# A graph kernel's count matrix: one table word per cell, and source one-hots made two units ahead

## The reference

```python
edge_index = jnp.stack([src, dst])
edge_index_t = jnp.stack([src, dst], axis=1)
x = _layernorm(x + _L0_gnn_ref(x, L0_gnn_W, L0_gnn_b, src, dst), axis=-1)
x = _layernorm(x + _L1_gnn_ref(x, edge_attr_128, edge_index_t, ...), axis=-1)
x = _layernorm(x + _L2_gnn_ref(x, edge_index, ...), axis=-1)
x = _layernorm(x + _L3_gnn_ref(x, src, dst, ...), axis=-1)
```

## Time and profile before

| | us |
|---|---|
| median of 3 runs | 8967.54 |
| lowest and highest run | 8958.18 to 8971.82 |
| profiled execution, whole time | 8958.67 |
| profiled execution, span of the core | 8956.9 |
| stage b, from its first VectorE operation to the end of loop two | 1383 to 3050 |
| loop one (32 turns) | 1450 to 2602 |
| loop two (16 lines) | 2602 to 3050 |

### The profile page before, as it was taken

How to read it: one execution, slowest core, us unless ns; L and a number is a source line. 1 busy time by engine, 2 the same in 40 slices (tenths; PEclk the granted TensorE clock), 3 DMA queues, 4 the chain that set the end, 5 groups by cost and what they waited for, 6 DMA issues and landing times. The chain is left out here.

```text
span 8956.9 us, 148669 instructions
## 1 busy us (share of the span) xinstructions
PE 6419.9 (72%) x40358; PEld 4410.9 (49%) x40359; DVE 4659.5 (52%) x13045; ACT 1832.2 (20%) x2602; POOL 3401.7 (38%) x3460
## 2 busy tenths in 40 slices
PE   0366503666666589999967777767777599968999
PEld 0255402444443245555546666656666355534555
DVE  6877745666766522222257777777777501022111
ACT  1222102333344310100013333223333100000000
POOL 0777776666663000000046666466666100000000
PEclk6688857888888799999989999889999799979999
DMA  0122202222223156777732222122222266635666
GB/s 16 46 70 72 62 1 61 89 85 85 92 92 79 50 166 175 185 177 187 191 74 50 50 50 51 43 53 50 50 51 50 74 188 190 191 101 164 192 190 182
DMA packets 871577, 901.11 MB, mean 101 GB/s; under 512 B 421539, under 2 KB 820226, under 8 KB 864867
## 3 DMA queue, kind: packets, MB, share of 16 engines
q1 hardware_dynamic: 753541, 637.16, 25.8%
q0 software_dynamic: 109664, 179.92, 8.9%
q10 hardware_dynamic: 8064, 80.29, 2.3%
HBM read 722.84 MB, written 93.87 MB: 91 GB/s over the span
## 5 line engine op out<-in xcount | busy, mean ns | idle before, releaser
L1919 POOL DMA_INDIRECT d_row_ring<-table_att,src_at x1664 | 1581.3, 950 | 819.3 <-issue 490.0
L2428 PE MATMUL psum<-e_a_ring,e_parts 128*128 128x448 bf16 x8232 | 1578.0, 353 | 82.9 <-DVE e_parts L2510 75.7
L2428 PEld LDWEIGHTS psum<-e_a_ring,e_parts 128*128 128x128 bf16 x8232 | 806.4, 98 | 823.9 <-issue 87.5
L775 POOL DMA_INDIRECT b_row_ring<-edge_attr,b_entry x896 | 894.9, 999 | 603.4 <-SPq L752 363.3
L794 PE MATMUL psum<-b_hot 128*128 x2920 | 672.7, 373 | 593.6 <-DVE b_hot L976 519.1
L353 POOL DMA_INDIRECT listed<-a_record,a_slot_no x832 | 866.0, 1041 | 314.6 <-issue 272.0
L1327 PE MATMUL psum<-c_a_ring,c_parts 128*128 128x448 bf16 x4116 | 811.6, 356 | 43.1 <-DMA c_a_ring<-adjacency 38.5
L1944 PE MATMUL psum<-edges_out,edges_in 128*128 128x120 f32 x4896 | 713.2, 307 | 179.9 <-ACT edges_in L2010 160.4
L1944 PEld LDWEIGHTS psum<-edges_out,edges_in 128*128 128x128 f32 x4896 | 661.0, 217 | 225.5 <-DVE edges_out L2103 203.9
L794 PEld LDWEIGHTS psum<-b_hot 128*128 x2920 | 293.8, 101 | 947.4 <-issue 826.7
L1960 PE MATMUL psum<-edges_out,edges_in 128*128 128x132 f32 x4896 | 651.2, 288 | 113.7 <-DVE edges_out L2157 113.7
(11 more groups left out here) (426 smaller groups left out, 7686.4 us busy)
## 6 DMA issues: line engine op xcount, KB each, us to landing
e_a_ring<-adjacency SPq DMA_DIRECT2D x1372, 224.0 KB, 2.8
c_a_ring<-adjacency SPq DMA_DIRECT2D x686, 224.0 KB, 2.9
adjacency<-b_line ACTq DMA_DIRECT2D x49, 1568.0 KB
a_cum<-edge_attr SPq DMA_DIRECT2D x103, 512.0 KB
d_row_ring<-table_att,src_at POOLq DMA_INDIRECT x1664
b_row_ring<-edge_attr,b_entry POOLq DMA_INDIRECT x896
listed<-a_record,a_slot_no POOLq DMA_INDIRECT x832
e_a_left<-adjacency_left SPq DMA_DIRECT2D x28, 224.0 KB, 3.2
```

The lines of the kernel that those rows point to most:

```text
L775: pool.indirect_dma_start(out=row_ring[:, u % 4, g, 0:D], out_offset=None, in_=a["edge_attr_128"], in_offset=bass.IndirectOffsetOnAxis(ap= ...
L1919: pool.indirect_dma_start(out=row_ring[:, u % 4, g, :], out_offset=None, in_=table_att[layer], in_offset=bass.IndirectOffsetOnAxis(ap=src_ ...
L2428: mm = nc.tensor.matmul(psum[:, 2 * (turn % 2) + v, 0:WIN], parts[:, piece, s, :], a_ring[:, s % SEVEN, v * WIN:(v + 1) * WIN], start=(s = ...
```

## The change

VectorE's share of stage b is rewritten in four points; TensorE, ScalarE, GpSimd and SyncE keep their instructions.

1. Two operations on one partition put the running count, shifted left by 19 bits, and the code of row 0 together into row 1 of `cell_row`. `spans_of` reads row 1 and takes column, number and count from one word; `befores` is no longer read by VectorE.
2. The source one-hots are made two pairs ahead: both pairs of `is_src` are filled before the first cells.
3. In the loops, the one-hot of a unit two pairs later follows directly on each addition (`turned_over`): add, hot, add, hot. The buffer that it overwrites is the one that the added unit has just finished with.
4. The wait for an addition stands ahead of the next addition and no longer behind each one. The codes load has eight words in loop one (six before) and six in loop two (four before).

```diff
             def spans_of(eng, q, n):
-                words = cell_row[0:1, 0, q:q + n] if isinstance(q, int) else cell_row[0:1, 0, bass.ds(q, n)]
-                return [(nc.s_assert_within(eng.snap(code >> 9), 0, COLS - 4, ...),
-                         nc.s_assert_within(eng.snap(code & 511), 1, COLS // 4, ...))
-                        for code in loaded(eng, words, 19)]
+                words = cell_row[0:1, 1, q:q + n] if isinstance(q, int) else cell_row[0:1, 1, bass.ds(q, n)]
+                return [(nc.s_assert_within(eng.snap((code >> 9) & 1023), 0, COLS - 4, ...),
+                         nc.s_assert_within(eng.snap(code & 511), 1, COLS // 4, ...),
+                         eng.snap(code >> 19))
+                        for code in loaded(eng, words, 30)]
...
+                st.by(V.tensor_scalar(cell_row[0:1, 1, :], cell_row[0:1, 2, :], 19, None, ALU.logical_shift_left))
+                st.settle(dve)
+                st.by(V.tensor_tensor(cell_row[0:1, 1, :], cell_row[0:1, 1, :], cell_row[0:1, 0, :], ALU.bitwise_or))
+                st.settle(dve)
...
-                def adds(i, pair):
-                    for h, (tile, _) in enumerate(pair):
-                        at = bass.ds(tile, 1)
-                        dve.wait_ge(s_sum, i * 2 + (h + 1))
-                        V.tensor_tensor(edges_out ..., ps_row[h], ALU.add).then_inc(s_added, 1)
-                        hold(dve, s_added, i * 2 + (h + 3), s_held_dve)
+                def add(i, h, code):
+                    at = bass.ds(code[0], 1)
+                    dve.wait_ge(s_sum, i * 2 + (h + 1))
+                    hold(dve, s_added, i * 2 + (h + 2), s_held_dve)
+                    V.tensor_tensor(edges_out ..., ps_row[h], ALU.add).then_inc(s_added, 1)
+
+                def turned_over(i, parity, pair, later):
+                    for h in range(2):
+                        add(i, h, pair[h])
+                        hot_of(parity, h, later[h])
...
-                hots(0, codes(0, 2))
-                cells(0, 0, 3, spans_of(dve, 0, 3), befores(dve, 0, 3))
+                for i in range(2):
+                    for h, code in enumerate(codes(2 * i, 2)):
+                        hot_of(i, h, code)
+                cells(0, 0, 3, spans_of(dve, 0, 3))
                 with dve.Fori(0, MORE) as s:
-                    pairs = codes(s * 4, 6)
+                    pairs = codes(s * 4, 8)
                     spans = spans_of(dve, s * NWIDE + 3, NWIDE)
-                    before = befores(dve, s * NWIDE + 3, NWIDE)
-                    hots(1, pairs[2:4])
-                    cells(s, 3, NWIDE, spans, before)
-                    adds(s * 2, pairs[0:2])
-                    hots(0, pairs[4:6])
-                    cells(s + 1, 0, 3, spans[NWIDE - 3:], before[NWIDE - 3:])
-                    adds(s * 2 + 1, pairs[2:4])
+                    cells(s, 3, NWIDE, spans)
+                    turned_over(s * 2, 0, pairs[0:2], pairs[4:6])
+                    cells(s + 1, 0, 3, spans[NWIDE - 3:])
+                    turned_over(s * 2 + 1, 1, pairs[2:4], pairs[6:8])
                 with dve.Fori(0, (NT - 1 - MORE) // 2) as i:
                     for k in range(2):
-                        pairs = codes(i * 4 + (4 * MORE + 2 * k), 4)
+                        pairs = codes(i * 4 + (4 * MORE + 2 * k), 6)
                         spans = spans_of(dve, (i * 2 + (MORE + k)) * NWIDE + 3, NWIDE)
-                        before = befores(dve, (i * 2 + (MORE + k)) * NWIDE + 3, NWIDE)
-                        cells(i * 2 + (MORE + k), 3, NWIDE, spans, before)
-                        hots(1 - k, pairs[2:4])
-                        cells(i * 2 + (MORE + k + 1), 0, 3, spans[NWIDE - 3:], before[NWIDE - 3:])
-                        adds(i * 2 + (2 * MORE + k), pairs[0:2])
+                        cells(i * 2 + (MORE + k), 3, NWIDE, spans)
+                        cells(i * 2 + (MORE + k + 1), 0, 3, spans[NWIDE - 3:])
+                        turned_over(i * 2 + (2 * MORE + k), k, pairs[0:2], pairs[4:6])
```

More of the change, by code:

```diff
@@ L100, in gnn_kernel @@
     EXACT = 256
-    assert MORE % 2 == 0 and NT % 2 == 1 and D == P and HEADS * CH == D and NW * WIN == NP and NWIDE == SEVEN and NT == SEVEN * SEVEN and N < NP and UNITS + NT < P * QJ and NT < 64
+    assert MORE % 2 == 0 and NT % 2 == 1 and D == P and HEADS * CH == D and NW * WIN == NP and NWIDE == SEVEN and NT == SEVEN * SEVEN and N < NP and UNITS + NT + 4 < P * QJ and NT < 64 and CELLS + NWIDE * COLS // 4 < 2048
     with ExitStack() as ctx:
@@ L713, in spans_of @@
             def spans_of(eng, q, n):
-                because = "a cell holds its first column and its number of four columns"
-                words = cell_row[0:1, 0, q:q + n] if isinstance(q, int) else cell_row[0:1, 0, bass.ds(q, n)]
-                return [(nc.s_assert_within(eng.snap(code >> 9), 0, COLS - 4, skip_runtime_bounds_check_because=because),
-                         nc.s_assert_within(eng.snap(code & 511), 1, COLS // 4, skip_runtime_bounds_check_because=because))
-                        for code in loaded(eng, words, 19)]
+                because = "a cell holds its first column, its number of four columns and how many came before"
+                words = cell_row[0:1, 1, q:q + n] if isinstance(q, int) else cell_row[0:1, 1, bass.ds(q, n)]
+                return [(nc.s_assert_within(eng.snap((code >> 9) & 1023), 0, COLS - 4, skip_runtime_bounds_check_because=because),
+                         nc.s_assert_within(eng.snap(code & 511), 1, COLS // 4, skip_runtime_bounds_check_because=because),
+                         eng.snap(code >> 19))
+                        for code in loaded(eng, words, 30)]
             def left_of(eng):
@@ L960, in _, with cell @@
                 dve.sem_inc(s_added, 2)
-                def cell(tile, window, span, at0):
-                    k0, n = span
+                def cell(tile, window, span):
+                    k0, n, at0 = span
                     with dve.Fori(0, n) as g:
@@ L978, in cell, with cells @@
                             last.then_inc(s_hot, 1)
-                def cells(s, first, end, spans, before):
+                def cells(s, first, end, spans):
                     for w in range(first, end):
-                        cell(s, slice(w * WIDE, (w + 1) * WIDE), spans[w - first], before[w - first])
+                        cell(s, slice(w * WIDE, (w + 1) * WIDE), spans[w - first])
                 def codes(q, n):
                     return codes_of(dve, out_pairs, UNITS - 1, q, n)
[L987 to L990, removed]
@@ L992, in adds @@
-                def adds(i, pair):
-                    for h, (tile, _) in enumerate(pair):
-                        at = bass.ds(tile, 1)
-                        dve.wait_ge(s_sum, i * 2 + (h + 1))
-                        V.tensor_tensor(edges_out[:, at, :].rearrange("p a f -> p (a f)"),
-                                        edges_out[:, at, :].rearrange("p a f -> p (a f)"), ps_row[h], ALU.add
-                                        ).then_inc(s_added, 1)
-                        hold(dve, s_added, i * 2 + (h + 3), s_held_dve)
@@ L1001, in _, with hot_of @@
-                hots(0, codes(0, 2))
-                cells(0, 0, 3, spans_of(dve, 0, 3), befores(dve, 0, 3))
+                def hot_of(parity, h, code):
+                    tile, unit = code
+                    V.tensor_tensor(is_src[:, parity, h, :, :], bc(key_src[:, bass.ds(unit * G, G)], 2, [P, G, P]),
+                                    bc(iota[:, bass.ds(tile * P, P)], 1, [P, G, P]), ALU.is_equal).then_inc(s_is_src, 1)
+                def add(i, h, code):
+                    at = bass.ds(code[0], 1)
+                    dve.wait_ge(s_sum, i * 2 + (h + 1))
+                    hold(dve, s_added, i * 2 + (h + 2), s_held_dve)
+                    V.tensor_tensor(edges_out[:, at, :].rearrange("p a f -> p (a f)"),
+                                    edges_out[:, at, :].rearrange("p a f -> p (a f)"), ps_row[h], ALU.add
+                                    ).then_inc(s_added, 1)
@@ L1018, in _ @@
-                        cells(i * 2 + (MORE + k), 3, NWIDE, spans, before)
-                        hots(1 - k, pairs[2:4])
-                        cells(i * 2 + (MORE + k + 1), 0, 3, spans[NWIDE - 3:], before[NWIDE - 3:])
-                        adds(i * 2 + (2 * MORE + k), pairs[0:2])
-                cells(NT - 1, 3, NWIDE, spans_of(dve, (NT - 1) * NWIDE + 3, NWIDE - 3),
-                      befores(dve, (NT - 1) * NWIDE + 3, NWIDE - 3))
-                adds(TWOS - 1, codes(2 * TWOS - 2, 2))
+                        cells(i * 2 + (MORE + k), 3, NWIDE, spans)
@@ L1026, in _ @@
+                        cells(i * 2 + (MORE + k + 1), 0, 3, spans[NWIDE - 3:])
+                        turned_over(i * 2 + (2 * MORE + k), k, pairs[0:2], pairs[4:6])
+                cells(NT - 1, 3, NWIDE, spans_of(dve, (NT - 1) * NWIDE + 3, NWIDE - 3))
+                for h, code in enumerate(codes(2 * TWOS - 2, 2)):
```

(4 more changed lines are left out.)

## The result

The changed kernel took 8977.26 us (median of 20 runs, 8969.66 to 8985.66) against 8964.86 us for the kernel before (20 runs beside them, 8952.36 to 8971.82): ratio 1.0015, 95% interval 1.0008 to 1.0022. It is 12.4 us slower, which by the prediction's bound of 0.2% is no difference. But the interval leaves out 1.0000: something costs 7 to 20 us. The prediction said +2. So the question is where some 12 us come from when the stage that was changed does what it should.

The account below looks back on a forecast made before the run. Loop one was taken as bound by the serial gather chain, loop two by TensorE's pace. Start +3.0, gathers +4 and TensorE's waits -5 gave +2 us on the median 8967.5, so 8969.5 us, range 8948 to 8990.

Parts of the forecast that it names:

- the prediction's bound of 0.2%: Whole kernel: 18 us, about what a measurement can tell from no change; no difference beyond it had chance 0.82.
- The start: Before the loops: table operations 1.1 us, two more source one-hots 2.4, less 0.5 of idle time: +3.0 us.
- the chain: Loop one: issue eight gathers, wait until they land, release the next; 91 units at 12.65 us, one after another.
- VectorE's gain: Both loops: 2.8 us less VectorE work per line; in loop one none of it reaches the end.
- the three terms of GpSimd: Loop one: 721.5 us issuing gathers, 194.5 between gathers, 233.1 at unit changes; together 1149 of 1152 us.
- Gathers held by the moved hots: Loop one, GpSimd: the second hot can catch the next gather; 0.06 us per pair of hots, +4 us.
- the rule it cites: Trainium skill: `tensor_tensor` with both inputs in SBUF blocks only GpSimd's reads; the gather term would be zero.
- Loop two: 16 lines paced by TensorE, cells 2.74 us apart; its waits for hots shrink by 5 us in all.
- The rival that VectorE bounds loop two: Loop two: VectorE sets the pace, so 45 us come out there and the kernel takes 8930 us; chance 0.07.
- two more words in the codes load: Both loops, VectorE: the longer load costs at most 0.47 us more per line.
- the sum: Whole kernel: +3.0 us start, +4 gathers, -5 TensorE's waits for hots, together +2 us.
- a change in a later stage: Behind the edited stage, untouched by the diff: could make the prediction wrong without its signs; given no size.

Follow-up runs that it names:

- e5: Kernel before, with SyncE releasing the slot of unit u+1 before it waits for unit u's rows: ratio 1.0173 to the kernel before.
- e6: Changed kernel, with SyncE releasing the slot of unit u+1 before it waits for unit u's rows: ratio 1.0172 to the kernel before.
- e12: Changed kernel with SyncE releasing the slot of unit u+1 before waiting for unit u's rows, run again on another chip: ratio 1.0194 to the kernel before.
- e10: Kernel before plus only 64 semaphore increments nobody waits for, ahead of VectorE's code behind the count-matrix stage: ratio 1.0006 to the kernel before.
- e1: Kernel before plus only 17 semaphore increments nobody waits for, ahead of VectorE's code behind the count-matrix stage: ratio 1.0016 to the kernel before.
- e7: Kernel before plus only 17 semaphore increments ahead of VectorE's later code, run again on a second chip: ratio 1.0015 to the kernel before.
- e11: Kernel before plus only 17 semaphore increments ahead of VectorE's later code, run again on a third chip: ratio 1.0012 to the kernel before.
- e9: The changed kernel again, unaltered, beside the kernel before on the same chip: 8968.98 against 8956.03 us, ratio 1.0015.
- e8: Changed kernel plus 47 semaphore increments, so VectorE's later code stands 64 instructions further on than in before: ratio 0.9991 to the kernel before.

## Why the prediction was right, and where it was not

*The start.* +3.0 us forecast; the first hot began at 1453.09 instead of 1449.87 us, +3.2. Right.

*Loop one.* Bound by the chain, VectorE's gain hidden: right by every sign it named. SyncE's waits are for rows, the three terms of GpSimd add to the loop within 1 us, and VectorE's wait for TensorE rose from 182.7 to 300.7 us (60 or more forecast). These are signs of the profile; the edit that was to test the chain (e5, e6, e12) never ran on such a chip. The forecast that the start's 3 us would be carried by the chain to its end is not borne out: by the order of TensorE's instructions the difference is within some 5 us of zero from 1651 us on.

*Gathers held by the moved hots.* +4 us forecast. Busy time beyond 0.944 us per gather is 716.6 - 726 x 0.944 = 31.3 us, against 34.3 before: -3. The term had the wrong sign, and is small. The prediction also says that by the rule it cites the term would be zero, and that the trace disagrees. That goes too far: the gather reads its row numbers (`b_entry`) from SBUF, and GpSimd's reads are what that rule, in the prediction's own words, has blocked. So the 1.97 us gather doesn't by itself speak against the rule.

*Loop two.* TensorE's cells are 2.73 us apart (forecast 2.74):

```profile
2841.27 1.77 PE L795 MATMUL psum<-b_hot 128*128 x8 [0.62 <-ACT psum L855]
...
2844.00 1.77 PE L795 MATMUL psum<-b_hot 128*128 x8 [0.96 <-DVE b_hot L981]
```

The loop is 3 us shorter, TensorE's waits at the hot tiles fell by 8.6 us (5 forecast), VectorE's for TensorE rose by 23.4 us (30 forecast, a miss). The rival that VectorE bounds loop two, with 45 us to gain, is out. One term of VectorE's own gain was mis-sized and is hidden all the same: two more words in the codes load were to cost 0.47 us, and the load went from 0.82 to 0.60 us in loop one and from 0.75 to 1.40 in loop two (medians). How little of this can be read off single profiles shows in e10: with before's own code its TensorE part of the stage takes 1658.5 us, in the profile of before 1676.3, in those of the changed kernel 1669.3 and 1663.0. The stage's net of -3.6 us is inside that spread.

*The step that failed* is the sum, which held only terms of the stage that is edited. It named a change in a later stage as what would make it wrong without its signs, and gave that nothing. The cost there is some 13 us by the three places; the whole difference measured is 12.4. Padding alone (e1, e7, e11) costs as much, though on the slower chips; before with 17 increments on a chip where it takes 8960 us is the run that is missing. So the forecast of no difference over 0.2% held, with 8969.5 us against 8977.26, but the direction of the +2 is luck: its terms are smaller than the one left out.

*Not settled.* The stage between 3158 and 4612 us is 10 us longer in the changed kernel's profile and 8 in e9's, 1 shorter in e10's. It comes in steps of 1 to 3 us at waits, with no longer interval between instructions that don't wait. One kernel's profiles differ there by 4 to 5 us (e1, e7 and e11; e6 and e12). Over all fourteen profiles it takes 1451 to 1456 us at shifts 0 and 64 (five of them) and 1455 to 1463 us at 17 (seven), 1463 at 6 and 1455 at 11. That leans to placement, with no place found for it; if so, the three places are not the whole price, and not all of the sum reaches the end. And the intervals of e9, e10 and the first 20 runs, each 6 to 8 us to either side, can't tell 12 us from 18.

## What to carry to other kernels

An edit that lengthens one engine's program also moves all of that engine's later code; with loops behind it, that alone was worth +4 to +18 us here, more than the edit's own effect. When a small change comes out a little slower or faster than its stage accounts for, run the old kernel padded by the same number of idle instructions before looking for a mechanism, and compare the intervals of the later loops one by one. And read a loop's bound again on each chip before spending an experiment on it.

## What the runs showed of the hardware

A loop's cost depends on where it stands in VectorE's program. The first search loop takes 0.22 us back to its head at shifts of 6, 11 and 17 instructions, 0.12 or 0.13 at 0 and 64, in all fourteen profiles; the second, 13 turns of the same function, takes 0.13 to 0.14 in all. In the long loop of the second pass one or two instructions of a turn come 0.09 to 0.11 us late (at a shift of 6 nothing is lost over the turn), and which ones depends on the shift; at 11 one of them is the branch at the end. Since it is the same place in every turn and on both kinds of chip, I take the supply of instructions to be the cause; that is argued, and no run showed it otherwise than through these times. In the changed stage itself VectorE's sequencer needs 0.34 us from the branch of loop one to its next instruction (median, 258 instructions a turn in before) and 3.0 us from that of loop two (502 a turn), before and after the change alike. It is part of the idle time at "issue" in the earlier trace rows.

On the chips of e1 to e8, e11 and e12 the kernels take 26 to 27% longer. The stages without gathers keep their length (the stretch of the scores takes 1696 to 1703 us on either kind). In the stages with gathers register and semaphore instructions of TensorE and VectorE, of some 0.05 us, take 0.7 us in bursts, often on both engines at once (in e7's loop one 191 of VectorE's 311 holds of over 0.6 us overlap one of TensorE's); none of ScalarE's there is over 0.07 us. What holds them these profiles don't say.
